# A decoder layer with routed experts: the passage from the shared product to the experts in another order, with two more buffers

## What is computed

```
x = x + attn(layernorm(x)); x = x + cross(layernorm(x), ctx)
h = rmsnorm(layernorm(x)) * norm_w               # 1600 tokens x 512
topk_w, topk_ids = top_k(softmax(h @ router_w.T), 4); topk_w /= sum(topk_w)
routed = sum over the 4: topk_w * (silu(h @ w1_gate[e]) * (h @ w1_up[e])) @ w2[e]
shared = (silu(h @ sg) * (h @ su)) @ sd
out = layernorm(x) + routed + shared
```

## Time and profile before

| | |
|---|---|
| median of 3 runs | 1201.46 us (1196.83 to 1204.07) |
| the profiled execution, its own time | 1205.08 us |
| its span, first to last instruction | 1203.3 us, 21050 instructions |
| PE busy | 1152.4 us (96%) |
| VectorE, ScalarE, GpSimd busy | 811.2, 596.3, 342.0 us (67%, 50%, 28%) |
| granted clock of PE, mean | 0.980 |

### The profile page before, as it was taken

How to read it: one execution, slowest core, us unless ns; L and a number is a source line. 1 busy time by engine, 2 the same in 40 slices (tenths; PEclk the granted TensorE clock), 3 DMA queues, 4 the chain that set the end, 5 groups by cost and what they waited for, 6 DMA issues and landing times. The chain is left out here.

```text
span 1203.3 us, 21050 instructions
## 1 busy us (share of the span) xinstructions
PE 1152.4 (96%) x7761; PEld 911.7 (76%) x7762; DVE 811.2 (67%) x1392; ACT 596.3 (50%) x1404; POOL 342.0 (28%) x279
## 2 busy tenths in 40 slices
PE   6989999999999999999999989999979999999995
PEld 3457677777767776777777667888769999999994
DVE  1255697888789878978887877542256666666661
ACT  1324554564455446545644534421136666666662
POOL 0011103211211221122112112222216666666543
PEclk9989999999999999999999998999989999999998
DMA  8441000000000000000000005032269999999964
GB/s 274 142 156 36 2 9 10 14 9 9 16 14 9 9 16 14 9 9 14 9 9 16 14 10 201 15 116 65 92 237 256 271 265 274 270 277 280 264 145 53
DMA packets 62598, 117.59 MB, mean 98 GB/s; under 512 B 10932, under 2 KB 14564, under 8 KB 62388
## 3 DMA queue, kind: packets, MB, share of 16 engines
q1 hardware_dynamic: 44820, 82.46, 20.4%
q0 software_dynamic: 17728, 34.44, 14.3%
HBM read 93.55 MB, written 28.13 MB: 101 GB/s over the span
## 5 line engine op out<-in xcount | busy, mean ns | idle before, releaser
L1483 POOL TENSOR_TENSOR rall<-qkv_var,phalf 100x17 f32<-100x17 f32 x16 | 49.2, 3072 | 410.1 <-DVE qkv_var L1163 410.1
L382 PE MATMUL QS<-xh,wh 128*128 128x256 f32 x512 | 147.7, 288 | 0.0
L384 PE MATMUL QS<-xh,wl 128*128 128x256 f32 x512 | 145.2, 284 | 0.0
L383 PE MATMUL QS<-xl,wh 128*128 128x256 f32 x512 | 145.2, 284 | 0.0
L1561 POOL DMA_INDIRECT out_rows<-work,idx x64 | 108.3, 1693 | 113.1 <-ACT work L1043 76.4
L382 PE MATMUL W<-wch,oth 128*100 128x512 f32 x256 | 105.0, 410 | 0.0
L383 PE MATMUL W<-wcl,oth 128*100 128x512 f32 x256 | 100.7, 393 | 0.0
L384 PE MATMUL W<-wch,otl 128*100 128x512 f32 x256 | 100.4, 392 | 0.0
L382 PEld LDWEIGHTS QS<-xh,wh 128*128 128x128 f32 x512 | 98.5, 192 | 1.2
L383 PEld LDWEIGHTS QS<-xl,wh 128*128 128x128 f32 x512 | 98.5, 192 | 1.2
L384 PEld LDWEIGHTS QS<-xh,wl 128*128 128x128 f32 x512 | 98.4, 192 | 0.0
(11 more groups left out here) (223 smaller groups left out, 2879.0 us busy)
## 6 DMA issues: line engine op xcount, KB each, us to landing
raw<-in_w SPq DMA_DIRECT2D x24, 1024.0 KB, 7.2
raw<-in_w SPq DMA_DIRECT2D x24, 512.0 KB, 9.3
work<-in_w SPq DMA_DIRECT2D x8, 1024.0 KB, 7.0
work<-in_w SPq DMA_DIRECT2D x8, 512.0 KB, 9.8
hx_rows<-h3x SPq DMA_DIRECT2D x16, 212.5 KB
h_columns<-h3s SPq DMA_DIRECT2D x16, 200.0 KB, 1.9
h3T<-h_columns SPq DMA_DIRECT2D x4, 800.0 KB, 9.8
out_rows<-ytiles POOLq DMA_DIRECT2D x16, 200.0 KB, 2.5
```

What stands on the lines that cost most here:

```text
L382: mm(dst, ah, bh, start=start, stop=False)
L383: mm(dst, ah, bl, start=False, stop=False)
L384: return mm(dst, al, bh, start=False, stop=stop)
L1483: return nc.gpsimd.tensor_tensor(out=dst, in0=src, in1=phalf[:, 0:src.shape[1]], op=ALU.pow)
```

## The change

Five edits, all between the router of the last batch row and the second expert.

1. Two more buffers, `last_sums`, behind the experts' split tensors: the third and fourth sum of group 3 go there and wait for no store (`sum_at`).
2. PE's order: chunk 5 stands ahead of the last batch row's transposes, chunk 6 ahead of its router, chunk 7 between router and ranks (it stood behind the first down product). The transposes of expert 0 stand ahead of `shared_outer(3)` and wait for `sh_act` 16.
3. VectorE's and ScalarE's order follows: chunk 5 before the router's results, chunk 6's product before the ranks, its low half behind the sums of group 0. At the end VectorE alternates: weights part 0, sum 0, rows of expert 0, sum 1, weights part 1, sums 2 and 3. ScalarE: weights part 0, rows, weights part 1.
4. `rows_high` of experts 0 and 1 wait for the sums of group 0 and 1 (`sh_y` 4 and 8) instead of for all 16; the weights of expert 1 wait for all 16.
5. SyncE loads expert 1's weights from `sh_u` 8 (the end of chunk 7) on, those of 2 and 3 from 16.

```diff
@@ -200,6 +200,13 @@
         ytile = [yt[0:T, HID * i:HID * (i + 1)] for i in range(2)]
+        last_sums, = turn(region + 17408, ("last_sums", 2 * HID, fp32))
+        ytile += [last_sums[0:T, HID * i:HID * (i + 1)] for i in range(2)]
+        def sum_at(g, t):
+            return t if g == 3 else t % 2
         h3l, w_sgl, w_sul, w_sdl = turn(h3_at, ("h3l", KC * NTOK, f32r), ("w_sgl", 2048, f32r), ("w_sul", 2048, f32r),
@@ -343,6 +350,8 @@
                 if e == 1:
+                    sp.wait_ge(s.sh_u, 8)
+                if e == 2:
                     sp.wait_ge(s.sh_u, 16)
@@ -684,39 +704,30 @@
             shared_inner(1, 0)
+            shared_inner(1, 1)
             normed_columns(NB - 1)
-            shared_inner(1, 1)
+            shared_inner(1, 2)
             router(NB - 1)
-            for g in range(4):
-                if 0 < g < 3:
-                    shared_inner(g + 1, 0)
-                    shared_inner(g + 1, 1)
-                if g == 0:
-                    shared_inner(1, 2)
-                    ranks(NB - 1)
-                shared_outer(g)
-                if g == 1:
-                    pe.wait_ge(s.sh_act, 10)
-                    pe.wait_ge(s.idx, 1)
-                    tr(qb[0][:, 0:2 * NE], ixf, ident[0:2 * NE, 0:2 * NE]).then_inc(s.ix_T, 1)
-                    pe.wait_ge(s.idx, 2)
-                if g < 3:
-                    if g > 0:
-                        shared_inner(g + 1, 2)
-                    shared_inner(g + 1, 3)
...
+            shared_inner(1, 3)
+            ranks(NB - 1)
+            shared_outer(0)
+            shared_inner(2, 0)
+            shared_inner(2, 1)
+            shared_outer(1)
+            pe.wait_ge(s.sh_act, 10)
+            pe.wait_ge(s.idx, 1)
+            tr(qb[0][:, 0:2 * NE], ixf, ident[0:2 * NE, 0:2 * NE]).then_inc(s.ix_T, 1)
+            pe.wait_ge(s.idx, 2)
+            shared_inner(2, 2)
+            shared_inner(2, 3)
+            shared_inner(3, 0)
+            shared_inner(3, 1)
+            shared_outer(2)
+            shared_inner(3, 2)
+            shared_inner(3, 3)
+            pe.wait_ge(s.sh_act, 16)
+            x_columns(0)
+            shared_outer(3)
@@ -1013,11 +1023,12 @@
             split_high("h2")
+            shared_inner(4)
             columns_out(NB - 1)
-            shared_inner(4)
+            shared_inner(5)
             top_exp(NB - 1)
-            for n in range(5, 8):
-                shared_inner(n)
+            shared_inner(6)
+            shared_inner(7)
             split_high("h3")
@@ -1027,10 +1038,14 @@
                 c = (slice(0, 2048), slice(2048, WX))[part]
+                if e == 1 and part == 0:
+                    act.wait_ge(s.sh_y, NB)
                 copy(wh[e % 2][:, c], slots_w[e % RING][:, c]).then_inc(m.wh, 1)
...
                 act.wait_ge(m.xT_ps, e + 1)
+                if e < 2:
+                    act.wait_ge(s.sh_y, 4 * (e + 1))
                 copy(xh[e % 2][:, :], QS[:, 0:1024]).then_inc(m.xh, 1)
@@ -1045,9 +1060,8 @@
             weights_high(0, 0)
+            rows_high(0)
             weights_high(0, 1)
-            act.wait_ge(s.sh_y, NB)
-            rows_high(0)
             for e in range(NE):
@@ -1355,13 +1369,15 @@
-            def shared_inner(n):
+            def shared_product(n):
...
                 tt(prod[:, :], shtmp[:, :], qb[2 + n % 2][:, 0:QW], ALU.mult).then_inc(s.sh_act, 1)
+            def shared_low(n):
                 dve.wait_ge(s.sh_high, n + 1)
@@ -1369,12 +1385,16 @@
-            def shared_rows(g):
-                for t in range(4):
+            def shared_inner(n):
+                shared_product(n)
+                shared_low(n)
+            def shared_rows(g, some=range(4)):
+                for t in some:
                     dve.wait_ge(s.sh_y_ps, 4 * g + t + 1)
-                    if 2 * g + t // 2 >= 1:
+                    if 2 * g + t // 2 >= 1 and sum_at(g, t) < 2:
                         dve.wait_ge((s.sh_st0, s.sh_st1)[t % 2], 32 * g + 16 * (t // 2))
-                    tt(ytile[t % 2], resid[0:T, 4 * HID * g + HID * t:4 * HID * g + HID * (t + 1)], wb[t][0:T, :], ALU.add)\
+                    tt(ytile[sum_at(g, t)], resid[0:T, 4 * HID * g + HID * t:4 * HID * g + HID * (t + 1)], wb[t][0:T, :], ALU.add)\
                         .then_inc(s.sh_y, 1)
@@ -1394,8 +1414,9 @@
             shared_inner(4)
+            shared_inner(5)
             routed(NB - 1)
-            shared_inner(5)
+            shared_product(6)
             ranked(NB - 1)
@@ -1403,26 +1424,22 @@
-            for g in range(4):
-                if g == 0:
-                    shared_rows(g)
-                    shared_inner(6)
-                    shared_inner(7)
-                if 0 < g < 3:
-                    shared_inner(4 * g + 4)
-                    shared_inner(4 * g + 5)
-                if g > 0:
-                    shared_rows(g)
-                if g == 1:
-                    dve.wait_ge(s.ix_T, 1)
-                    nc.vector.tensor_copy(idx[:, :], qb[0][:, 0:2 * NE]).then_inc(s.idx, 1)
-                if 0 < g < 3:
-                    shared_inner(4 * g + 6)
-                    shared_inner(4 * g + 7)
-                if g == 0:
-                    split_low("h3")
-                    dve.wait_ge(s.ix_ld, 16 * FAST)
-                    nc.vector.tensor_copy(ixf, ixr).then_inc(s.idx, 1)
+            shared_rows(0)
+            shared_low(6)
+            shared_inner(7)
+            split_low("h3")
+            dve.wait_ge(s.ix_ld, 16 * FAST)
+            nc.vector.tensor_copy(ixf, ixr).then_inc(s.idx, 1)
+            shared_inner(8)
+            shared_inner(9)
+            shared_rows(1)
+            dve.wait_ge(s.ix_T, 1)
+            nc.vector.tensor_copy(idx[:, :], qb[0][:, 0:2 * NE]).then_inc(s.idx, 1)
+            for n in range(10, 14):
+                shared_inner(n)
+            shared_rows(2)
+            shared_inner(14)
+            shared_inner(15)
@@ -1438,8 +1455,11 @@
             weights_low(0, 0)
+            shared_rows(3, [0])
+            rows_low(0)
+            shared_rows(3, [1])
             weights_low(0, 1)
-            rows_low(0)
+            shared_rows(3, [2, 3])
             for e in range(NE):
@@ -1540,7 +1560,7 @@
                     pool.wait_ge(s.sh_y, 4 * g + t + 1)
-                    pool.dma_start(dst, ytile[t % 2]).then_inc((s.sh_st0, s.sh_st1)[t % 2], 16)
+                    pool.dma_start(dst, ytile[sum_at(g, t)]).then_inc((s.sh_st0, s.sh_st1)[t % 2], 16)
```

More of the change, by code:

```diff
@@ L667, in shared_outer, with x_columns @@
                     last.then_inc(s.sh_y_ps, 1)
+            def x_columns(e):
+                u = e % AHEAD
+                pe.wait_ge(s.gath[u], 16 * FAST * (e // AHEAD + 1))
+                if e > 0:
+                    pe.wait_ge(m.xT, e)
+                for j in range(FAST):
+                    for k in range(KC):
+                        last = tr(QS[:, 256 * k + P * j:256 * k + P * (j + 1)], Xg[u][j][:, P * k:P * (k + 1)], ident[:, :])
+                last.then_inc(m.xT_ps, 1)
             cross_queries(NB, True)
@@ L746, in outer @@
                     last.then_inc(m.y_ps, 1)
-            x_columns(0)
             for e in range(NE):
```

## The result

| | before | after |
|---|---|---|
| median of 20 runs each | 1202.32 us (1195.38 to 1220.12) | 1193.62 us (1187.81 to 1210.15) |
| span of the profiled execution | 1203.3 us | 1185.9 us |
| ratio after to before | | 0.9923, 95% interval 0.9901 to 0.9944 |

The change saves 0.77%, or 9.3 us with an interval of 6.7 to 11.9. The forecast was 11.05 us and 1190.4 us, range 1183.5 to 1196.5. The ratio leaves out runs more than 1.5% above the fastest of their kernel (two of before, four of after), so it isn't quite the ratio of the two medians. The one profiled execution of the changed kernel is the fastest of its 20 runs (1187.81 us), and its span is 17.4 us shorter than that before.

What follows compares the result with a forecast made beforehand. PE, busy nearly all the time, was taken as the bound. 10.7 (passage) + 0.35 (head) = 11.05 us off the median 1201.46 gave 1190.4 us, range 1183.5 to 1196.5.

Steps and rivals of the forecast that it cites:

- P: Forecast gain of the passage from the last shared product to expert 2's transposes: 8.73 + 1.97 = 10.7 us.
- transposes free: Passage: expert 0's transposes, 0.8 us, run inside the 1.90 us PE waits before group 3's down product and cost nothing.
- outer(3) at full clock: Passage: group 3's down product takes 11.16 us at full clock and ends at 878.60.
- The clock at 866: Before group 3's down product: transposes cut the gap into 0.7 and 0.2 us, so no clock fall, a 1.6 us loss.
- The head's new order: Chunks 5 to 7 around the last batch row's steps: 4.6 us gained less a 1.0 gap before chunk 6, 3.6.
- The collision: Head: expert 1's load delays the list scatter to 5.4 us; PE idles 1.65 before chunk 9, clock falls, 1.6.
- H: Forecast gain of the head, from the last batch row's transposes to chunk 9: 3.6 - 1.65 - 1.6 = 0.35 us.
- Expert 1's early load at nothing for the passage: Passage: expert 1's weights come from the head, no gain counted; those of 2 and 3 are wanted only after 889.
- No collision: Rival, head: scatter lands in time, 1187.2 us, or PE idles 1.65 at full clock, 1188.8; chance 0.30.
- The clock in outer(3): Rival, passage: two gaps act like one of 1.90, clock falls in group 3's down product; 1192.0 us; chance 0.20.
- `xl` late: Rival, passage: expert 0's `xl` late again behind weight halves waiting for ScalarE; gain 5 us, 1196.5; chance 0.05.
- Slower experts: Rival, expert stage: scatters meet loads in a worse phase, each expert 0.5 us longer, 1206.5 us; chance 0.04.

Runs made afterwards that it cites:

- e6: The changed kernel with the head's order undone and all three weight loads from chunk 15 on; chunk 4 to expert 2's transposes 114.68 us, ratio to before 0.9916.
- e2: The changed kernel with expert 0's transposes back behind outer(3); chunk 4 to expert 2's transposes 120.11 us.
- e5: The kernel before with the head's new order alone, no early load; chunk 4 to expert 2's transposes 121.87 us, ratio to before 0.998.
- e1: The changed kernel with expert 1's weights loaded from chunk 11 on, not chunk 7; chunk 4 to expert 2's transposes 111.11 us, ratio to before 0.9895.
- e4: The kernel before with expert 1's weights loaded from chunk 7 on, expert 2's from chunk 15; chunk 4 to expert 2's transposes 123.05 us.
- e7: The changed kernel with chunk 6's low half and chunk 7's product behind two sums of group 0, not four; chunk 4 to expert 2's transposes 111.11 us.
- e9: The kernel before with the two added buffers alone; chunk 4 to expert 2's transposes 123.36 us.
- e10: The kernel before with expert 0's transposes ahead of outer(3) alone; chunk 4 to expert 2's transposes 123.30 us.
- e8: The changed kernel with e1's and e7's edits and product 4 ahead of h2's low half; chunk 4 to expert 2's transposes 109.85 us, ratio to before 0.9872.

## Why the prediction was right

- **P, 10.7 us, measured 10.74; the passage alone takes 10.70 off M (e6).** Each step held: transposes free, outer(3) at full clock, `xl` 5.9 us early (5.5 said), expert 1's transposes behind outer(3) without a wait, 6.6 us from there to the next.
- **The clock at 866.** The choice to read two gaps with transposes between as short was right; e2 shows the other side, 1.5 us.
- **The head's new order, 3.6 us.** Without the collision it measures 3.51 in e5, and 3.53 in e1 (125.38 less 111.11 less P). 1.6 us of it is the fall of the clock behind the 3.00 us gap. It was in the trace that the sum used and in three of the four others with that gap, but not in e4. Against a trace without it the head would have been worth some 2 us, so the close match is luck in part.
- **The collision, 3.25 us.** It measures 3.74 (114.85 less 111.11): scatter 5.6 us (5.4 said), gap 1.93 (1.65 said), a fall of the clock behind it as said. This is the term that was mis-sized; H came out at -0.21 us where 0.35 was forecast: 0.28 of that by the gap, 0.2 by the clock's fall (1.8 us where 1.6 was said), the rest by the head's 3.52 where 3.6 was said.
- **Expert 1's early load at nothing for the passage.** Right in the new order (e6), wrong in the old, where e4 gains 1.2.
- **The rivals.** None of the four came about. No collision: the scatters did land late, though e1 shows what it would have given. The clock in outer(3): it stayed at 1.00. `xl` late: it was 5.9 us early. Slower experts: M's end to the span's end is the same within 0.4 us. The rule of "DMA: Bandwidth & Descriptors", section Queues, rings and completion order in the Trainium skill, that queues take turns packet by packet, would have let the scatters through; here, with expert 1's load, the last one took 5.6 us and without it 2.9. The queues may take turns all the same; no run here separates the turns from the landing, and it is the landing that the chain waits for.
- **The time.** 9.3 us by the ratio for 11.05 forecast, 10.53 in M. The last two differ by H's half microsecond; the first two differ by less than the interval of the ratio.

## What to carry to other kernels

A transfer that nobody waits for is not free: ask which small transfers share its time and which engine stands in a queue behind them. Here one 1.57 MB load, moved to a place where nothing needed its data yet, cost 3.7 us through scatters, a load, two stores, two sums and a product. Where an engine's queue mixes work that waits for stores with work that the bottleneck needs, put the needed work first: that, with the transposes moved, was the gain at the passage's end, and e7's repair at the head. More buffers gave 0.5 us once the order was right, and 2.0 before.

## What I had not expected of the hardware

A gap of PE of the same length and in the same place does not always bring the clock down: the 3.00 us before the last batch row's transposes did in the kernel before, e6, e9 and e10 (chunk 5 took 5.98 to 6.03 us) and not in e4 (4.49). The first batch rows show it more: M starts at 764.1 to 765.4 us in five of the twelve executions and at 767.7 to 771.8 in the other seven, with the same code ahead of it. The five early ones are all variants of the changed kernel, but so are e1, e5 and e6, which start late, and the timed ratios agree with M and not with M plus 6 us (e8: 15.4 us with an interval of 10.7 to 20.0, M 15.5). The earlier start makes up 6.5 of the 17.4 us of the profiled pair. That it is also much of the spread between runs of one kernel is likely and not shown: a run's mean granted clock broadly goes with its time (0.989 in the changed kernel's run of 1187.8 us, 0.980 in that of 1210.2).
